# Token pairs of mixed tiles added to the output in two transfers instead of after a joining product

## What is computed

```python
x = x + tanh(g_xattn[0]) * xattn(ctx_512, layernorm(x), Wq, Wk, gamma_raw)
x = x + tanh(g_ffn[0]) * ffn(layernorm(x), ...)

# ffn, x is [2048, 512]
shared = silu(x @ shared_gate_w) * (x @ shared_up_w) @ shared_down_w
top_val, top_idx = top_k(x @ router_w, 2)                  # 2 of 8 experts
probs = zeros.at[arange(T)[:, None], top_idx].set(sigmoid(top_val))
gu = einsum('etd,edf->etf', probs.T[:, :, None] * x[None], gate_up_w)
h = silu(gate) * up
out = shared + einsum('eti,eid->etd', h, down_w).sum(axis=0)
```

## Time and profile before

| | us |
|---|---|
| median of 3 runs (lowest, highest) | 395.9 (395.59, 397.62) |
| the profiled execution | 397.11 |
| its span | 395.4 |
| TensorE busy | 367.4 (93%) |
| VectorE busy | 256.2 (65%) |
| ScalarE busy | 212.1 (54%) |
| GpSimd busy | 142.1 (36%) |

### The profile page before, as it was taken

The page is one execution under the profiler, slowest core; times in us unless marked ns, Lnnn a source line. Parts: engine busy times, 40 slices in busy tenths (PEclk is TensorE's granted clock), DMA queues, the critical chain, the costliest instruction groups (busy, mean ns, idle before and its releaser), DMA issues.

```text
span 395.4 us, 7266 instructions
## 1 busy us (share of the span) xinstructions
PE 367.4 (93%) x2372; PEld 233.0 (59%) x2374; DVE 256.2 (65%) x858; ACT 212.1 (54%) x406; POOL 142.1 (36%) x114
## 2 busy tenths in 40 slices
PE   8957889989999999999999999999999999999970
PEld 4313478557845588457875475757545644567750
DVE  1799999999999689960846793645547654623310
ACT  3595788476653686435220575554556565652320
POOL 2200220030533342222215265463656655644422
PEclk9986999999999999999999999999999999999996
DMA  7999971166657633449241755544535353644244
GB/s 218 383 388 382 389 242 37 27 195 182 189 108 170 200 64 34 72 112 206 35 53 35 128 79 90 103 77 85 87 78 91 72 86 76 107 61 87 44 55 53
DMA packets 29357, 51.18 MB, mean 129 GB/s; under 512 B 4614, under 2 KB 7942, under 8 KB 29318
## 3 DMA queue, kind: packets, MB, share of 16 engines
q0 software_dynamic: 9920, 22.16, 34.1%
q1 hardware_dynamic: 19110, 28.40, 20.8%
q10 hardware_dynamic: 288, 0.13, 0.1%
HBM read 28.60 MB, written 22.09 MB: 128 GB/s over the span
## 4 chain that ended last, share of the span: by engine, by line
PE 71%; ACT 8%; DMA 7%; DVE 7%; issue 3%; POOL 1%; SPq 1%; POOLq 1%; DVEq 0%; ACTq 0%
PE gate_up L1317 25%; PE down L1367 15%; PE gate_up L1326 8%; PE gate_up L1332 6%; PE down L1358 4%; PE turned_x L1295 4%; DMA out_dram<-y_sb,idx 3%; ACT junk L713 3%; PE front L1274 2%; DMA xs<-in_x_dram 2%; DMA out_dram<-y_sb,tmp 1%; DMA out_dram<-tmp,idx 1%; PE front L1182 1%; ACT x L750 1%; ACT sim L708 1%
## 5 line engine op out<-in xcount | busy, mean ns | idle before, releaser
L1317 PEld LDWEIGHTS gate_up<-xT,w_shgu 128*128 128x128 f32 x1024 | 117.6, 192 | 11.7 <-issue 10.4
L1317 PE MATMUL gate_up<-xT,w_shgu 128*128 128x128 f32 x1024 | 121.0, 276 | 1.5 <-ACT xT L761 1.1
L565 POOL DMA_INDIRECT xg<-x_rows,idx x34 | 52.2, 1534 | 43.5 <-DMA x_rows<-payl 13.5
L589 POOL DMA_INDIRECT out_dram<-y_sb,idx x20 | 35.9, 1793 | 54.0 <-DMA out_dram<-y_sb,idx 20.9
L815 ACT ACTIVATE y_sb<-down,gates 128x512 f32<-128x512 f32 x42 | 28.8, 687 | 36.5 <-PE down L1367 24.9
L1367 PE MATMUL down<-w_dn,hT 128*128 x100 | 47.0, 596 | 0.0
L2045 DVE COPY sim<-w_gu 128x2048 f32 x36 | 42.1, 1221 | 1.9 <-issue 1.0
L713 ACT ACTIVATE junk<-sim,probe 128x512 int8<-128x512 f32 x44 | 31.2, 712 | 16.8 <-DVE probe L1730 9.9
L2053 DVE COPY w_shgu<-w_gu 128x2048 f32 x16 | 20.0, 1249 | 26.6 <-PE gate_up L1317 17.7
L826 ACT COPY xs<-w_dn 128x1024 f32 x36 | 36.0, 1045 | 2.0 <-issue 1.7
L2074 DVE SCALAR_TENSOR_TENSOR h<-gate_up,p_t,silu 128x256 f32<-128x256 f32 x18 | 8.7, 482 | 42.9 <-ACT silu L784 33.9
(11 more groups left out here) (241 smaller groups left out, 535.0 us busy)
## 6 DMA issues: line engine op xcount, KB each, us to landing
w_gu<-in_L_ffn_gate_up_w_dram SPq DMA_DIRECT2D x8, 1024.0 KB
xs<-in_x_dram SPq DMA_DIRECT2D x4, 1024.0 KB, 7.7
w_dn<-in_L_ffn_down_w_dram SPq DMA_DIRECT2D x8, 512.0 KB
out_dram<-xs SPq DMA_DIRECT2D x4, 1024.0 KB, 6.0
x_rows<-x SPq DMA_DIRECT2D x4, 1024.0 KB, 4.7
out_dram<-y_sb POOLq DMA_DIRECT2D x16, 256.0 KB
w_gu<-in_ctx_dram SPq DMA_DIRECT2D x4, 256.0 KB, 5.8
xg<-x_rows,idx POOLq DMA_INDIRECT x34
```

Of the source, the lines that this page charges most:

```text
L565: G.indirect_dma_start(out=xg[:, t % XG, :], out_offset=None, in_=x2_rows[0:2 * N, :] if t < EARLY else x2_rows[:, :], in_offset=bass.Indi ...
L589: G.indirect_dma_start(out=out[0:2 * N, :] if t < EARLY else out[:, :], out_offset=bass.IndirectOffsetOnAxis(ap=rows, axis=0), in_=y_at(j) ...
L1317: mm = TE.matmul(g_b[j % 2][:, f * P:(f + 1) * P], w_shgu[:, c, f * P:(f + 1) * P], xT[:, x_slot(j), c], start=(c == 0), stop=(c == DC - 1))
```

## The change

Five things are changed together.

- The joining product (fold), its copy (folded_y) and the nine matrices are gone. The first transfer of a mixed tile (scatter) takes y as y_of leaves it, with idx_s as before. A second transfer (scatter_doubles) takes the same y with idx_d, in which only the second rows of a token point at the output and all others at dump rows. It waits until the tile's first transfer has landed and counts in doubles_out.
- Three waits come with it: a mixed tile's scatter, from the second one on, waits for the second transfer of the mixed tile before it; tile 32's scatter waits for all nine; and y_of waits for the second transfer, too, where its buffer's previous user was a mixed tile.
- The mixed tiles are 9, 11, 13, 15, 18, 21, 24, 27 and 30 instead of 9, 12, 15, 18, 20, 22, 24, 26 and 28.
- In GpSimd's list the second transfer stands behind the scatter of the next tile for tiles 9, 11, 13 and 30, and behind the scatter of the second next tile for 15, 18, 21, 24 and 27.
- STAGED holds only tile 33. Fifteen uniform tiles lose the copy of weights and the weighing of rows; they multiply with x as the stationary side, and get a turn_h and a copy of hT.

```diff
-    MIXED = (9, 12, 15, 18, 20, 22, 24, 26, 28)
+    MIXED = (9, 11, 13, 15, 18, 21, 24, 27, 30)
...
-    STAGED = [t for t in range(EARLY + 1, MT) if t not in MIXED]
+    STAGED = [33]
...
+        idx_d = tmp[:, 3, 48:48 + MIX].bitcast(I32)
...
                 if t == PAIR:
                     rows = idx_p
+                    pool.wait_ge(doubles_out, 16 * MIX)
                     pool.wait_ge(scatter_ready, 1)
                 if m is not None:
-                    pool.wait_ge(folded, m + 1)
+                    if m:
+                        pool.wait_ge(doubles_out, 16 * m)
                     pool.wait_ge(scatter_ready, 1)
...
+            def scatter_doubles(t):
+                m = MIXED.index(t)
+                pool.wait_ge(scattered, 16 * CHAIN.index(t) + 16)
+                G.indirect_dma_start(out=out[:, :], out_offset=bass.IndirectOffsetOnAxis(ap=idx_d[:, m:m + 1], axis=0),
+                                     in_=y_at(job_of("M", t)), in_offset=None, compute_op=ALU.add
+                                     ).then_inc(doubles_out, 16)
...
                 if k is not None and is_m(k):
                     act.wait_ge(scattered, 16 * CHAIN.index(JOBS[k][1]) + 16)
+                    if mixed_at(k) is not None:
+                        act.wait_ge(doubles_out, 16 * mixed_at(k) + 16)
...
-            def folded_y(j):
-                act.wait_ge(fold_ps, mixed_at(j) + 1)
-                A.copy(y_at(j), f_b[0][:, :]).then_inc(folded, 1)
...
-            def fold(j):
-                m = mixed_at(j)
-                pe.wait_ge(y_done, j + 1)
-                pe.wait_ge(twins_done, 3)
-                if m:
-                    pe.wait_ge(folded, m)
-                TE.matmul(f_b[0][:, :], fold_m[:, m * P:(m + 1) * P], y_at(j), start=True,
-                          stop=True).then_inc(fold_ps, 1)
...
-                    V.tensor_scalar(fold_m[:, m * P:(m + 1) * P], others, row_f[:, m:m + 1], None, ALU.is_equal)
...
+                V.tensor_scalar(idx_d, unused[:, 0:MIX], dump, None, ALU.add)
```

More of the change, by code:

```diff
@@ L374, in flamingo_gated_block @@
         rows_weighed = sem("rows_weighed")
-        folded = sem("folded")
+        doubles_out = sem("doubles_out")
         gu_ps = sem("gu_ps")
@@ L502, in _ @@
             sp.wait_ge(scattered, 16 * MT)
+            sp.wait_ge(doubles_out, 16 * MIX)
         @block.gpsimd
@@ L1035, in _ @@
             y_of(29)
-            stage_down(2, 2)
-            stage_down(2, 3)
+            turned_h(30)
+            stage_down(3, 0)
+            stage_down(3, 1)
             silu_of(31)
@@ L1050, in _ @@
             y_of(32)
-            stage_down(3, 2)
-            stage_down(3, 3)
+            turned_h(33)
+            stage_down(4, 2)
+            stage_down(4, 3)
             silu_of(34)
@@ L1119, in _ @@
             y_of(44)
-            folded_y(44)
+            turned_h(45)
+            stage_down(8, 2)
+            stage_down(8, 3)
             silu_of(46)
@@ L1371, in down @@
                     pe.wait_ge(twins_done, 3)
-                    mm = TE.matmul(y_b[j % 2][:, :], fold_m[:, MIX * P:(MIX + 1) * P], joined, start=False, stop=True)
+                    mm = TE.matmul(y_b[j % 2][:, :], join_m, joined, start=False, stop=True)
                 mm.then_inc(y_ps, 1)
@@ L1594, in _ @@
             down(25)
-            up(27, 25)
+            turn_h(26)
+            up(27)
             turn_rows(12)
             down(26)
+            turn_h(27)
             up(28)
@@ L1604, in _ @@
             down(28)
-            up(30, 28)
+            turn_h(29)
+            up(30)
             turn_rows(15)
             down(29)
+            turn_h(30)
             up(31)
@@ L1614, in _ @@
             down(31)
-            up(33, 31)
+            turn_h(32)
+            up(33)
             turn_rows(18)
             down(32)
+            turn_h(33)
             up(34)
@@ L1659, in _ @@
             down(44)
-            up(46, 44)
+            turn_h(45)
+            up(46)
             turn_rows(31)
             down(45)
+            turn_h(46)
             up(47)
@@ L2013, in find_twins @@
                 if k == 2:
-                    both = fold_m[:, MIX * P:(MIX + 1) * P]
+                    both = join_m
                     link(V.tensor_scalar(both, f_b[0][:, P:2 * P], row_p[:, 0:1], None, ALU.is_equal))
@@ L2317, in _ @@
             stage_up(4, 3)
-            gate(35)
-            stage_full(21)
-            weight_of(21)
-            gate(36)
-            weight_of(22)
+            weight_of(17)
+            gate(32)
+            weight_of(18)
+            gate(33)
+            weight_of(19)
+            gate(34)
             stage_up(5, 0)
@@ L2326, in _ @@
             stage_up(5, 3)
+            weight_of(20)
+            gate(35)
+            weight_of(21)
+            gate(36)
+            weight_of(22)
             gate(37)
-            stage_full(23)
-            weight_of(23)
-            gate(38)
-            weight_of(24)
             stage_up(6, 0)
@@ L2335, in _ @@
             stage_up(6, 3)
+            weight_of(23)
+            gate(38)
+            weight_of(24)
             gate(39)
-            stage_full(25)
             weight_of(25)
             gate(40)
-            weight_of(26)
             stage_up(7, 0)
@@ L2349, in _ @@
             weight_of(28)
+            gate(43)
             stage_up(8, 0)
@@ L2353, in _ @@
             stage_up(8, 3)
-            gate(43)
-            stage_full(29)
             weight_of(29)
```

142 lines of the change are left out of this document (68 added, 74 removed).

## The result

The changed kernel takes 408.9 us (median of four, 406.1 to 410.8) against 395.9 before: a ratio of 1.031, interval 1.026 to 1.036. It is slower, by 13 us where 7.6 were forecast; that is inside the range of 397 to 411 but above the 400 to 407 in which the forecast itself had put it. The profiled execution took 407.4 us, with a span of 405.7; that is 10.3 us more than the span before.

The account below looks back on a forecast made before the run. Scatters were to replace TensorE as the bound: 23 steps of 152.4 us move the span from 395.4 to 402.1, 1 us of stretched issues makes 403.0; that 7.6 more on the median 395.9 gives 403.5 us, range 397 to 411.

Parts of the forecast that it names:

- What becomes the bound: The chain of scatters on GpSimd was to replace TensorE: 19.6 us for three tiles against TensorE's 18.3.
- Which steps are long: Scatters of mixed tiles 11 to 30 and tile 32 start 7.75 or 8.4 us after the scatter before, others 5.62.
- the three kinds: Steps from tile 9's scatter to tile 32's: 14 of 5.62 us, three of 7.75, six of 8.4.
- The landing: Time from a second transfer's issue until it has landed, put at 5.15 us from the last two scatters before.
- Stretched issues: GpSimd's issues taking longer beside VectorE's weight copies: nothing to 1.8 us each, 1 us in all on the chain.
- the plain sum: The 23 steps from tile 9's scatter to tile 32's without stretched issues, together 152.4 us.
- each run is done when the group's last scatter starts or soon after: Reason for only 1 us of stretching: VectorE's runs of four weight copies would mostly end before meeting scatters.
- TensorE's own gain: Nine joining products (9.7 us) go, fifteen transpositions (3.3 to 5.7 us) come: TensorE's sum 4 to 6 us less.
- The second: Rival: landings are quicker than the pair's, so the scatter chain only just replaces TensorE; 394 to 398; chance 0.10.
- The third: Rival: TensorE stays the bound, second transfers landing before their buffer is needed; faster, about 389; chance 0.08.
- The first: Rival: second transfers land later, one us more in each of nine steps; 412; chance 0.17.
- The fourth: Rival: ScalarE's and VectorE's new order makes a wait in front of the next gate product; 404 to 408; chance 0.05.

Follow-up runs that it names:

- e1_early: Changed kernel with the second transfers of tiles 15, 18, 21, 24 and 27 placed behind the next tile's scatter instead of the second next; 398.2 us, ratio 1.0047.
- e2_no_second: Changed kernel without the nine second transfers and the waits for them, so it leaves out part of the result; 386.7 us, ratio 0.975.
- e7_small_copies: Changed kernel with VectorE's gate/up weight copies cut to 16 columns from the second mixed tile on, so wrong weights there; 399.8 us, ratio 1.0074.
- e0_again: The changed kernel unaltered, run and profiled once more on the chip of other follow-up kernels; 405.1 us, ratio 1.024, span 402.7.
- e3_turned_only: Kernel before, with only tile 33's weights copied and fifteen uniform tiles using x as stationary side with h transposed; joining products kept; 395.9 us, ratio 0.9994.
- second set: The executions of e0_again: the changed kernel unaltered, run again with other kernels between; 405.1 us, ratio 1.024.
- e5_spread: e1_early with mixed tiles at 9, 11, 14, 17, 19, 22, 25, 28, 30 and weight copies split over two tiles where there is room; 393.7 us, ratio 0.992.
- e8_buffers: e5_spread with the three y buffers taken in turn from job 24 on instead of 26; 396.7 us, ratio 0.998.
- e6: e1_early with VectorE's four weight copies of a mixed tile split two and two over two tiles at the five wide places; 395.3 us, ratio 0.996.
- e9: e8_buffers with mixed tiles at 9, 12, 14, 17, 19, 22, 24, 27 and 29; 395.9 us, ratio 0.996.
- e11_one_port: e9 with most weight copies done in full as a multiplication by 1.0 that also writes a sum; 392.2 us, ratio 0.989.
- e10_even_small: e9 with gate/up weight copies cut to 16 columns from the second mixed tile on, so wrong weights there; 390.9 us, ratio 0.985.

## Why the prediction was right, and where its sizes were off

- **What becomes the bound: right.** Scatters took TensorE's place; e1_early and e2_no_second show that it is the second transfers' place and waits, not load and not TensorE.
- **Which steps are long: right. How long: each a little too long.** Without collisions in e7_small_copies the three kinds came to 5.5, 7.6 to 8.0 and 7.9 to 8.3 us (mean 8.05) against 5.62, 7.75 and 8.4 (plain steps, those that wait for a second transfer alone, those whose buffer waits as well). The landing, put at 5.15 us, was 5.3 by the median of the first profile and 5.1 in e0_again and e7_small_copies. From ScalarE's end to the next scatter I took 0.65 us, and it was 0.27. The 0.65 were misread: the scatter at 384.67 waited for the landing of the one before it, at 379.02 + 4.88 = 383.90, and 0.77 us from landing to next start is the plain step's own; that ScalarE ended at 384.02 was chance. The whole from tile 9 to 32 is 148.8 us in e7_small_copies, against 152.4.
- **Stretched issues: right in kind, mis-sized.** I took "1 us in all". It was 4 to 7 us on the chain. This and the 3.6 us by which the plain sum was too high offset each other, so that 153.4 us in all for that stretch came near the 155.9 and 152.7 measured: the closeness is in part luck. Three steps from one mixed tile to the next were not 19.6 us but 19.5 to 20.6 in the first profile. In the first profile the scatters of tiles 9, 12, 13, 16, 20, 23 and 26 together took 5.0 us more than 1.58 each. The wrong step was "each run is done when the group's last scatter starts or soon after". I read it so: while scatters lag behind TensorE, copies that follow TensorE's pace drift across them, and on a chain without slack each collision counts in full. By the Trainium skill ("SBUF — State Buffer", Who interferes with whom) the prediction had put up to 10 us, 1.2 for each of nine meetings of a second transfer with a run. The rows after show 0.2 to 1.7 us for a meeting, in seven scatters of the first profile and five of the second. The second transfers themselves were all issued in 1.55 to 1.57 us: it was the scatters that met the copies. The truth lay between.
- **TensorE's own gain: under-sized.** A sum 4 to 6 us less was forecast. In e2_no_second TensorE was busy for 8.0 us less than before, and the time was 9.5 us less. e3_turned_only shows where: the fifteen turned tiles add only 0.5 us to TensorE's busy time and nothing to the kernel's, where 3.3 to 5.7 us had been put. So nearly all that the nine joining products took comes free, some 1 us each.
- **Rivals.** The second, that landings are quick, fell: no second transfer landed sooner than 4.7 us in either profile of the changed kernel. The third, that TensorE stays the bound, fell as argued. The first (1 us more in each step) gave 412, for a reason that is not found: the medians of the second transfers' landings lie within 0.15 us of the 5.15 that were put. The fourth (a wait made by ScalarE's and VectorE's new order, 404 to 408) fits the time of the second set, as it was said to be hard to tell by time alone. The rows speak against it as the cause: from tile 18 on, the steps into mixed tiles end with a landing or with ScalarE's copy that waited for one, and the longest wait of TensorE for VectorE's h behind them is 0.9 us. A small part of the 4 to 7 us that e7_small_copies wins may be of this kind. Of the rest, 408.9 minus 403.5, some 1.5 us is the distance of the median from the profiled execution; the 405.1 of the second set shows how far this kernel's time moves.

## What to carry to other kernels

When two serial chains are within ten per cent of each other, ask of an edit which chain it lengthens, and count the waits behind a moved transfer on every engine, above all those for its buffer. A transfer that nobody waits for is nearly free (0.5 us each for the five of e1_early, between the scatters of tiles 15 and 30), and the same transfer one place later cost 1.4 us more here, 6.9 us over five. On a chain that has no slack, count each collision with a neighbour in full, and put work that collides in a form that does not.

## What the runs showed of the hardware

TensorE's granted clock fell after TensorE had stood still for a few microseconds, and stayed low when work was there again. The stretches around the step into tile 18 in the changed kernel (start:end us, length, busy us of PE, PEld, DVE, ACT, POOL, granted clock, DMA share, GB/s):

```profile
296.00:301.00 5.00, 1.46 (x7) 0.70 (x5) 0.00 (x0) 0.00 (x0) 2.19 (x2) 1.00 0.90 147
301.00:302.00 1.00, 0.00 (x0) 0.00 (x0) 0.00 (x0) 0.87 (x2) 0.00 (x0) 0.94 0.08 29
302.00:304.00 2.00, 1.78 (x2) 0.84 (x3) 0.00 (x0) 1.94 (x3) 1.60 (x2) 0.50 0.01 4
304.00:306.00 2.00, 2.00 (x9) 0.81 (x11) 0.57 (x3) 1.24 (x4) 1.00 (x1) 0.68 0.97 121
306.00:308.00 2.00, 2.00 (x20) 0.53 (x18) 0.00 (x0) 2.00 (x4) 0.32 (x1) 1.00 0.49 143
```

```profile
302.22 3.49 PE L1375 MATMUL down<-w_dn,hT 128*128 x4 [4.76 <-ACT hT L812]
```

After a gap of 4.76 us the clock is at 0.50, the lower of its two levels, and the four passes of a down product took 3.49 us, against 1.88 in the next such row. In e5_spread a gap of 3.00 us was followed by 3.77 us for the same work, 0.63 instead of 0.38 for a transposition and 4.61 instead of 3.64 for a gate/up product. So these gaps cost TensorE some 2 to 3 us more than their length, an estimate from these rows. Nothing of it shows in the time of these kernels, since scatters bounded them: e8_buffers, without gap and low clock, was not faster than e5_spread.

A transfer of 256 KB issued 1.9 us behind another landed 5.1 to 5.4 us after its own issue, against 4.5 to 6.0 (median 4.9) for the scatters, all in the first profile of the changed kernel, with a gather behind both. In e0_again it was 4.7 to 5.3 us. So with two or three in flight the later one landed some 0.2 to 0.4 us later than the scatters' median.

Most kernels that the scatters bound differ more from one execution to the next: 4.7 us between the fastest and the slowest of the changed kernel's four, 4 to 5 us in e5, e6, e8 and e9, against 2.6 us in nineteen executions of the kernel before. It was 1.3 us in e7_small_copies, without collisions, and in e11_one_port, with few. But in e10_even_small, without collisions too, it was 3.5 us in four executions. That the copies meet the scatters in other places from one execution to the next was seen in the two profiles of the changed kernel; e10 shows that it can't be all of the spread.
